# Two attention blocks instead of three, and eight of eleven sorted expert tiles returned through memory

## The chip, the cores and the metric

The kernel runs on one core of a Trainium2 chip. The metric is the device time of one execution in microseconds (us); the table below gives the median of three timed executions. TensorE is called PE, its weight loads PEld, VectorE DVE, ScalarE ACT, GpSimd POOL and SyncE SP, as in the profile. Each engine runs its own instructions in the order in which they are written, and semaphores order the engines among each other.

## The reference, cut to what matters

For 64 images, a small vision tower. The patches of each image go through a convolution; nine patches form a window and four windows a picture. Local attention (one query per window over its nine patches) gives four rows per image, and global attention over those four rows gives a class row. With one more token that makes six tokens of 256 numbers per image (384 rows in all, three tiles of 128). Then follow one transformer layer (layernorm, causal attention with 16 heads of 8 query numbers and 16 value numbers, output projection, residual) and a mixture of experts:

```
logits = layernorm(h) @ gate_w                       # 8 experts
p, idx = top_k(softmax(logits), 2);  p /= p.sum()
out_e  = (silu(x @ gate_e) * (x @ up_e)) @ down_e    # 512 hidden numbers
h      = h + sum over the two picks of p * out_e[idx]
```

All numbers are float32. Where accuracy asks for it, a float32 number is split into a high and a low part (names HI and LO), and a product is three matmuls (HI*HI, HI*LO, LO*HI).

## The kernel before, in words

**Up to the router.** The convolution of 18 tiles (six groups of three) feeds keys and values (`keys_values`, line 686: one pass of 512 columns makes the 256 key and the 256 value numbers of a tile). DVE scores windows (`window_scores`, L1778 and L1780; for the last three tiles one position at a time, `position_scores`, L1764 and L1766), takes the softmax and multiplies the values (`value_products`, L484). PE adds these nine products while it transposes them (`second_aggregate`, L754), projects (`local_rows`, L782), and makes the three row tiles in banks 6, 7 and 5: `patch_rows(0)` and `patch_rows(1)` (L799), and, after the softmax over the windows and its products (`global_scores` L809, `global_values` L819, `global_aggregate` L829), `class_rows` (L843). Each row tile is normalised (`row_moments`; ACT or DVE writes `inn`), turned (`turn_in`, L642), and multiplied by the query, key and value weights (`qkv`, L908). PE's order is written out by hand: for instance `qkv_cls` and the whole of `patch_rows(0)` stand before `second_aggregate`.

The attention among six tokens is done on DVE in blocks of queries. `BLOCKS` = (0,3), (3,5), (5,6): queries 0 to 2 over 3 keys (9 pairs), queries 3 and 4 over 5 keys (10 pairs), query 5 over 6 keys (6 pairs). For a block, `attention_products` (L505) multiplies 64 numbers for each pair, `att_dots` (L1984) adds them by head, `att_scores` (L1990, L1993) subtracts the maximum, ACT takes the exponential (L1380), `att_weights` (L2001, L2004, L2006) divides, and `token_values` (L496, on DVE and POOL) weighs the values. PE sums and turns these (`turn_context`, L754), projects them, and the router follows.

**From the router on.** Expert 0 is dense: all rows go through it. The picks of experts 1 to 7 are sorted by expert into 11 tiles of 128 rows (`SLOT_TILES`). Two tiles are gathered by one-hot matmuls; POOL scatters all rows into a memory tensor by six indirect transfers (`scatter`, L1647), and the other nine tiles are read from there into a ring of six (`tile_rows`, L466). The tile loop (lines 1169 to 1180 on PE) does in step s:

- `tile_gate_up(s)`: 12 matmuls of 512 columns (L1101) with expert weights split by ACT (`tile_weights_hi`, L1400) and DVE (`tile_weights_lo`, L2020);
- `rows_turn(s+1)` (L1086), then `tile_out(s-1)`, the down projection (L1121);
- `give_back(s-2)` (L1134): six matmuls with the one-hot matrix `back` that POOL makes (`way_back`, L1655), which add a tile's HI and LO rows into the three row tiles of the sum, in banks 4, 7 and 2. It needs `out_hi` on ACT (L1490) and `out_lo` on DVE (L2210);
- `hidden_turn(s)` (L1110), which needs ACT's silu (L1475) and DVE's `tile_product` (L2204); ACT's `hidden_copy` (L1482) follows.

SP loads the weights of a tile in two parts, 1024 KB (`tile_a`, L553) and 512 KB (`tile_b`, L560), into a ring of three. `tile_a(t)` waits until tile t-3 is split, `tile_b(t)` until `tile_out(t-3)` is done. After the loop PE adds the residual and the dense expert's rows (`add_repeated`, L1154, L1156), then the last tile (`last_give_back`: three HI matmuls, and three LO matmuls that wait for `out_lo(10)`), and ACT and DVE copy the sums out.

## Time and profile before

| what | value |
|---|---|
| three timed executions | 207.58, 206.12, 205.95 us (median 206.12) |
| the profiled execution | 204.24 us, of which the span of its instructions is 202.4 us |
| busy PE, PEld, DVE, ACT, POOL | 190.9, 166.0, 139.8, 105.4, 79.1 us |
| bytes moved | 32.90 MB |

The profiled execution is 1.88 us below the median of the timed ones, and its span leaves out 1.84 us around the first and the last instruction. All rows below are of that one execution, in us from the start of its span.

### The profile page before, as it was taken

The numbers are of one execution on the slowest core, as the hardware profiler recorded it, in microseconds if no ns is written. First come the engines' busy times: TensorE is split into PE (matmuls) and PEld (weight loads), VectorE is DVE, ScalarE is ACT, GpSimd is POOL, SyncE is SP. The second block draws the span as 40 slices with busy tenths as digits, with TensorE's granted clock in tenths as the row PEclk, the third lists the DMA queues.
The fourth block names the chain that finished last, engine by engine and source line by source line (L and its number), as shares of the span: only waits on it lengthen the run. The fifth ranks groups of instructions, "written<-read, shape, count | busy, mean of one in ns | idle before, by whom it ended". The sixth has DMA issues, their size and how long they took to land.

```text
span 202.4 us, 3427 instructions
## 1 busy us (share of the span) xinstructions
PE 190.9 (94%) x1123; PEld 166.0 (82%) x1123; DVE 139.8 (69%) x344; ACT 105.4 (52%) x233; POOL 79.1 (39%) x112
## 2 busy tenths in 40 slices
PE   8999999999999997999968799999999999999991
PEld 8898989998897875877747599888878888888881
DVE  1787983585999997745798869396496676766311
ACT  4366492645427444543842551473486676767331
POOL 6235076464474040359355536790032222102220
PEclk9999999999999999999999999999999999999998
DMA  6999997000491000000002900217999987923003
GB/s 214 358 389 367 361 343 236 2 0 3 143 410 70 3 0 0 0 2 0 3 0 71 429 21 2 102 55 195 419 394 377 360 284 290 317 96 108 0 0 78
DMA packets 10349, 32.90 MB, mean 163 GB/s; under 512 B 1222, under 2 KB 5788, under 8 KB 8668
## 3 DMA queue, kind: packets, MB, share of 16 engines
q1 hardware_dynamic: 8140, 29.53, 40.3%
q10 hardware_dynamic: 1904, 2.37, 3.6%
q0 software_dynamic: 288, 0.79, 1.1%
q8 instruction: 9, 0.15, 0.3%
q14 instruction: 8, 0.07, 0.1%
HBM read 30.05 MB, written 2.64 MB: 161 GB/s over the span
## 4 chain that ended last, share of the span: by engine, by line
PE 75%; DVE 18%; issue 3%; ACT 2%; POOL 0%; DVEq 0%; ACTq 0%; POOLq 0%
PE bank L1101 15%; PE bank L1121 9%; PE bank L597 8%; PE bank L695 6%; PE bank L618 6%; PE bank L1029 4%; PE bank L1134 4%; PE bank L1039 3%; PE bank L1110 2%; DVE stats L1724 2%; PE bank L642 2%; PE bank L605 2%; DVE kv_rows L1778 1%; DVE vprod L484 1%; DVE split L1882 1%
## 5 line engine op out<-in xcount | busy, mean ns | idle before, releaser
L1101 PE MATMUL bank<-split 128*128 128x512 f32 x132 | 33.4, 401 | 0.1
L1655 POOL TENSOR_SCALAR split<-token_row,window 128x384 fp32r<-128x384 f32 x11 | 15.1, 1372 | 46.5 <-PE bank L1134 46.5
L1101 PEld LDWEIGHTS bank<-split 128*128 128x128 f32 x132 | 24.0, 188 | 5.3 <-issue 0.3
L695 PE MATMUL bank<-split 128*128 128x512 f32 x108 | 26.5, 397 | 0.0
L1559 POOL TENSOR_TENSOR rstd<-veps,mhalf 128x1 f32<-128x1 f32 (+2 forms) x17 | 14.3, 844 | 28.1 <-DVE veps L1731 27.9
L2020 DVE TENSOR_TENSOR split<-raw,split 128x512 fp32r<-128x512 f32 x28 | 18.4, 695 | 6.7 <-ACT split L1400 6.6
L695 PEld LDWEIGHTS bank<-split 128*128 128x128 f32 x108 | 19.8, 188 | 3.9
L597 PE MATMUL bank<-split 128*128 128x256 f32 (+1 forms) x180 | 22.7, 285 | 0.0
L597 PEld LDWEIGHTS bank<-split 128*128 128x128 f32 (+1 forms) x180 | 22.1, 191 | 0.2
L1400 ACT CAST split<-raw 128x512 fp32r<-128x512 f32 x28 | 16.7, 619 | 2.8 <-DMA raw<-ffn_w 2.8
L1247 ACT ACTIVATE kv_rows<-bank,rstd 128x512 f32<-128x512 f32 x18 | 12.1, 688 | 10.1 <-PE bank L695 9.3
L2204 DVE TENSOR_TENSOR kv_rows<-bank,kv_rows 128x512 f32<-128x512 f32 x11 | 7.6, 691 | 12.3 <-PE bank L1101 9.1
L1579 POOL TENSOR_TENSOR window<-window,pe_rows 128x256 f32<-128x256 f32 x14 | 11.7, 838 | 9.3 <-ACT pe_rows L1196 8.6
L1196 ACT COPY pe_rows<-bank 128x256 f32<-128x256 f32 x18 | 6.3, 373 | 16.1 <-PE bank L597 15.5
L618 PE MATMUL bank<-split 128*128 128x256 f32 (+1 forms) x90 | 12.6, 296 | 0.0
L2020 DVE TENSOR_TENSOR split<-kv_rows,split 128x512 fp32r<-128x512 f32 x16 | 11.1, 733 | 1.9 <-ACT split L1400 1.9
L618 PEld LDWEIGHTS bank<-split 128*128 128x128 f32 (+1 forms) x90 | 11.7, 201 | 0.5 <-DVE split L1866 0.2
L1724 DVE BATCH_NORM_STATS2 stats<-pe_rows 128x6 f32<-128x256 f32 x18 | 6.5, 414 | 8.3 <-ACT pe_rows L1196 8.1
L1134 PE MATMUL bank<-split 128*128 128x256 f32 x60 | 10.5, 311 | 0.0
L1211 ACT CAST split<-raw 128x384 fp32r<-128x384 f32 (+1 forms) x15 | 6.7, 510 | 6.0 <-DMA raw<-xb 4.0
L1400 ACT CAST split<-kv_rows 128x512 fp32r<-128x512 f32 x16 | 9.5, 621 | 0.4 <-PE bank L1101 0.4
L1475 ACT ACTIVATE kv_rows<-bank 128x512 f32<-128x512 f32 x11 | 6.6, 599 | 5.7 <-PE bank L1101 5.7
(282 smaller groups left out, 401.7 us busy)
## 6 DMA issues: line engine op xcount, KB each, us to landing
raw<-ffn_w SPq DMA_DIRECT2D x7, 1024.0 KB, 7.7
kv_rows<-ffn_w SPq DMA_DIRECT2D x4, 1024.0 KB, 5.4
raw<-xa SPq DMA_DIRECT2D x5, 768.0 KB
raw<-ffn_w SPq DMA_DIRECT2D x7, 512.0 KB, 7.4
kv_rows<-ffn_w SPq DMA_DIRECT2D x4, 512.0 KB, 5.9
tok<-tok_w SPq DMA_DIRECT2D x1, 1536.0 KB, 12.5
raw<-ffn_w SPq DMA_DIRECT2D x1, 1536.0 KB, 6.8
expert_rows<-zero_row SPq DMA_DIRECT2D x1, 1419.0 KB, 15.8
```

The source lines that it names most:

```text
L597: mm = pe.matmul(bank[b][:, 0:C], xs[0:n, g % 2, px, a:a + P], cws[0:n, pw, k, :], start=(k == 0 and m == 0), stop=(k == len(KCH) - 1 and ...
L618: mm = pe.matmul(bank[GT * g + j][:, 0:C], xs[0:n, g, px, a:a + P], cws[0:n, pw, k, :], start=(k == 0 and m == 0), stop=last)
L695: mm = pe.matmul(bank[b][:, :], lns[:, g % 2, px, a:a + P], wkvs[:, pw, aw:aw + 2 * C], start=(c == 0 and m == 0), stop=(c == CC - 1 and m ...
L1101: mm = pe.matmul(bank[half][:, :], xst[:, s % 2, px, c * P:(c + 1) * P], tile_aws[s % 2][:, piece, pw, :], start=(c == 0 and m == 0), stop ...
L1121: mm = pe.matmul(bank[6][:, 0:C], hcols[s % 2][:, q * P:(q + 1) * P], b_ring[ring(s)][:, q, :], start=(q == 0), stop=(q == FQ - 1))
L1134: mm = pe.matmul(bank[SUM_BANK[j]][:, 0:C], back[:, s % 2, j * P:(j + 1) * P], eo[:, s % 2, px, :], start=(s == 0 and px == HI), stop=False)
L1247: act.activation(kv_rows[:, 0:wt + 2:wt + 1, n, :], bank[b][:, :].rearrange("p (k c) -> p k c", k=2), ACT.Identity, scale=rstd[:, k, i - G ...
L1400: act.copy(tile_aws[s % 2][:, piece, HI, :].rearrange("p (q n) -> p q n", q=FQ), a_ring[ring(s)][:, :, piece * P:(piece + 1) * P]).then_in ...
L1559: pool.tensor_tensor(rstd[0:parts, k, 0:n], veps[0:parts, k, 0:n], mhalf[0:parts, 0:n], ALU.pow).then_inc(rstd_done, 1)
L1579: pool.tensor_tensor(redsum[:, wt, :], pe_rows[:, wt, 0, :] if n == 1 else redsum[:, wt, :], pe_rows[:, wt, n, :], ALU.add).then_inc(sum_s ...
L1655: pool.tensor_scalar(back[:, s % 2, :], token_row[:, :], xr[:, s % ROW_RING, ROW_TOKEN:ROW_TOKEN + 1], None, ALU.is_equal).then_inc(back_d ...
L2020: dve.tensor_tensor(tile_aws[s % 2][:, piece, LO, :].rearrange("p (q n) -> p q n", q=FQ), a_ring[ring(s)][:, :, piece * P:(piece + 1) * P] ...
```

## The change

There are two attention blocks, (0,3) and (3,6); the second has 18 pairs, so there are 27 pairs in place of 25. Contexts are still turned in three lots: tokens 1, 2, 0; then 5; then 3 and 4. The last three tiles' keys are made ahead of their values (`last_keys`, `last_values`), and their scores go as one `window_scores(1, 2)`. PE's order up to the attention is another: `second_aggregate` comes straight behind the first window's rows, with `global_scores(0)` inside; `patch_rows` and parts of the global values fill in; and all turns of the three row tiles and all `qkv` products stand behind `class_rows`. `in1` is normalised on DVE, and POOL makes the roots of `in0` and `in1` behind three weight splits.

Of the 11 sorted tiles the first eight (`FAR`) are no longer added by matmuls. ACT writes their weighted rows to a ring of three buffers, SP stores each tile (131 KB) to a new memory tensor `far_out`, and after the eighth POOL fetches each token's two rows by six indirect transfers of 128 rows (a pick in a later tile fetches a row of zeros). DVE adds the fetched rows to the row tiles. Tiles 8 to 10 go by `give_back` as before. There is one more small table on POOL, one more 131 KB store of zeros, and the load semaphores of the patch groups are shared by ring slot.

```diff
-BLOCKS = [(0, 3), (3, 5), (5, 6)]
+BLOCKS = [(0, 3), (3, 6)]
+CTX_TOKENS = ((1, 2, 0), (3, 4), (5,))
+FAR = SLOT_TILES - 3
+OUT_RING = 3
+ORDER_BACK = (2, 1, 0)
...
         def tile_rows(eng, s):
             if s >= ROW_RING:
-                eng.wait_ge(back_done, s - ROW_RING + 1)
-                eng.wait_ge(tile_out_split, s - ROW_RING + 1)
+                eng.wait_ge(tile_out_hi, s - ROW_RING + 1)
...
+            sp.dma_start(far_out[FAR * P:, :], zero_row[:, 0:C]).then_inc(zeroed, 16)
...
+            def far_write(s):
+                sp.wait_ge(tile_out_hi, s + 1)
+                sp.dma_start(far_out[s * P:(s + 1) * P, :], out_ring[:, s % OUT_RING, :]).then_inc(far_written[s % OUT_RING], 16)
...
                 if s + 2 < SLOT_TILES:
                     tile_a(s + 2)
                 tile_b(s)
+                if s - 3 < FAR:
+                    far_write(s - 3)
...
-            keys_values_group(5)
+            last_keys()
+            first_aggregate()
+            last_values(0)
+            local_begin(0)
+            last_values(1)
+            class_keys_mean()
+            local_rows(0)
+            last_values(2)
...
-            first_aggregate()
-            local_begin(0)
-            class_keys_mean()
-            local_rows(0)
             local_columns(0)
+            second_aggregate()
+            local_begin(1)
+            local_rows(1)
+            global_value(0, 0)
+            local_columns(1)
+            global_value(0, 1)
+            global_scores(1)
             patch_begin(0)
             patch_rows(0)
-            global_scores(0)
+            for c in range(CC):
+                mm = global_value(1, c)
+            mm.then_inc(filled[4], 1)
+            patch_begin(1)
+            patch_rows(1)
+            global_aggregate()
+            class_begin()
+            class_rows()
+            turn_in(0)
             pe.wait_ge(att_in, 16)
             pe.wait_ge(tok_cols, 1)
             qkv("qkv_cls")
-            second_aggregate()
-            local_begin(1)
-            local_rows(1)
-            turn_in(0)
-            local_columns(1)
-            patch_begin(1)
-            global_scores(1)
-            patch_rows(1)
-            global_values()
+            turn_in(1)
             tile_qkv(0, "qkv0", 0)
-            global_aggregate()
-            class_begin()
-            class_rows()
-            turn_in(1)
+            turn_in(2)
             tile_qkv(0, "qkv0", 1)
-            tile_qkv(1, "qkv1", 0)
-            turn_in(2)
-            tile_qkv(1, "qkv1", 1)
+            tile_qkv(1, "qkv1")
             tile_qkv(2, "qkv_pool")
...
             def tile_out(s, between=None):
-                pe.wait_ge(*((tile_out_split, s) if s else (hid_done, DENSE * FQ)))
+                if s > FAR:
+                    pe.wait_ge(tile_out_split, s - FAR)
+                else:
+                    pe.wait_ge(*((tile_out_hi, s) if s else (hid_done, DENSE * FQ)))
...
-                if s > 1:
+                if s - 2 >= FAR:
                     give_back(s - 2)
...
             def add_repeated():
                 pe.wait_ge(repeat_done, 2)
-                pe.wait_ge(acc_done, RT + 1)
+                pe.wait_ge(returned, 2)
                 pe.matmul(bank[SUM_BANK[2]][:, 0:C], repeat, acc[:, 2, :], start=False, stop=False)
-                pe.wait_ge(acc_done, 2 * RT)
+                pe.wait_ge(returned, 4)
...
+            h_copy(0)
             h_copy(1)
-            in_normalise(1)
+            in_normalise(0)
+            hT_copy(0)
             h_copy(2)
             hT_copy(1)
+            qkv_copy("qkv_cls")
+            copy_pair(2, "in2", hT[:, T - 1, :, :, :].rearrange("p c s b -> p c (s b)"))
             qkv_copy("qkv0")
-            copy_pair(2, "in2", hT[:, T - 1, :, :, :].rearrange("p c s b -> p c (s b)"))
             qkv_copy("qkv1")
+            qkv_copy("qkv_pool")
             attention_exp(0)
-            qkv_copy("qkv_pool")
             tile_weights_hi(0, 0)
-            attention_exp(2)
+            attention_exp(1)
             tile_weights_hi(0, 1)
-            attention_exp(1)
...
             def out_hi(s):
                 act.wait_ge(tile_down, s + 1)
                 wait_rows(act, s)
-                if s >= 2:
-                    act.wait_ge(given, s - 1)
+                if s < FAR:
+                    if s >= OUT_RING:
+                        act.wait_ge(far_written[s % OUT_RING], 16 * (s // OUT_RING))
+                    act.activation(out_ring[:, s % OUT_RING, :], bank[6][:, 0:C], ACT.Identity,
+                                   scale=xr[:, s % ROW_RING, ROW_WEIGHT:ROW_WEIGHT + 1]).then_inc(tile_out_hi, 1)
+                    return
...
-            for s in range(SLOT_TILES):
-                way_back(s)
+            way_back(FAR)
+            way_back(FAR + 1)
+            pool.wait_ge(far_step, 2)
+            for k in range(OUT_RING):
+                pool.wait_ge(far_written[k], 16 * len(range(k, FAR, OUT_RING)))
+            for j in ORDER_BACK:
+                for i in range(PICKS):
+                    pool.indirect_dma_start(returned_rows[:, i, j, :], None, far_out,
+                                            bass.IndirectOffsetOnAxis(ap=far_row[:, i, j:j + 1], axis=0)).then_inc(rows_back, 16)
+            way_back(FAR + 2)
...
             attention_products(dve, 0, ("qkv_cls", "qkv0")).then_inc(qk_dve, 1)
             att_dots(0)
             att_scores(0)
-            attention_products(dve, 1, ("qkv_cls", "qkv0", "qkv1")).then_inc(qk_dve, 1)
             att_weights(0)
-            attention_products(dve, 2, ("qkv_pool", "qkv1")).then_inc(qk_dve, 1)
-            att_dots(2)
-            att_scores(2)
+            attention_products(dve, 1, ("qkv_cls", "qkv0", "qkv1", "qkv_pool")).then_inc(qk_dve, 1)
             att_dots(1)
             att_scores(1)
-            att_weights(2)
-            att_wait(2, ATT)
-            token_values(dve, 5, SHARE, T).then_inc(dve_values, 1)
             att_weights(1)
             att_wait(1, ATT)
+            token_values(dve, 5, SHARE, T).then_inc(dve_values, 1)
             values(4)
...
+            def add_returned(j):
+                dve.wait_ge(acc_done, 2 * RT)
+                dve.wait_ge(rows_back, PICKS * RT * 16)
+                for i in range(PICKS):
+                    if i:
+                        dve.wait_ge(returned, 2 * ORDER_BACK.index(j) + i)
+                    dve.tensor_tensor(acc[:, j, :], acc[:, j, :], returned_rows[:, i, j, :], ALU.add).then_inc(returned, 1)
...
+                if s == 2:
+                    far_rows()
-                if s:
+                if s > FAR:
                     out_lo(s - 1)
+            for j in ORDER_BACK:
+                add_returned(j)
             out_lo(SLOT_TILES - 1)
```

## Rows read from the trace of the kernel before

**Rows 1.** The page, part 1: busy time of each engine.
```profile
PE 190.9 (94%) x1123; PEld 166.0 (82%) x1123; DVE 139.8 (69%) x344; ACT 105.4 (52%) x233; POOL 79.1 (39%) x112
```
**Rows 2.** Chain that ended last, in time: start, length, instruction.
```profile
20.04 5.39 PE bank L597 x45
...
72.78 4.25 PE bank L695 x18
...
83.58 1.97 PE bank L754 x18
...
94.25 1.15 PE bank L843 x4
...
107.20 1.58 DVE window L496 x2
...
163.64 0.71 PE bank L1134 x6
```
**Rows 3.** Timeline of one steady tile step: start, length, engine, line.
```profile
161.75 1.89 PE L1121 MATMUL bank<-kv_rows,loT 128*128 128x256 f32 x8
161.79 0.69 DVE L2204 TENSOR_TENSOR kv_rows<-bank,kv_rows 128x512 f32<-128x512 f32 x1 [0.99 <-PE bank L1101]
...
163.27 0.88 PEld L1134 LDWEIGHTS bank<-split 128*128 128x128 f32 x6
...
163.68 0.47 ACT L1490 ACTIVATE split<-bank,window 128x256 fp32r<-128x256 f32 x1 [0.32 <-PE bank L1121]
164.09 0.46 PEld L1110 LDWEIGHTS bank<-con,kv_rows 128*128 128x128 f32 x4
...
164.54 3.02 PE L1101 MATMUL bank<-split 128*128 128x512 f32 x12
```
**Rows 4.** Timeline up to the attention, 78 to 108 us.
```profile
80.38 2.70 DVE L484 TENSOR_TENSOR vprod<-kv_rows,pn 128x768 f32<-128x768 f32 x3
...
97.52 0.38 ACT L1375 COPY kv_rows<-bank 128x256 f32<-128x256 f32 x1
...
97.96 1.44 PEld L908 LDWEIGHTS bank<-att,tok 128*128 128x128 f32 x8
...
100.24 0.83 DVE L505 TENSOR_TENSOR vprod<-kv_rows 128x640 f32<-128x640 f32 x1
...
101.58 0.23 DVE L2006 TENSOR_TENSOR kv_rows<-kv_rows,r 128x72 f32<-128x72 f32 x1
...
103.55 0.89 DVE L1984 TENSOR_REDUCE kv_rows<-vprod 128x80 f32<-128x720 f32 x1
...
105.71 0.69 DVE L496 TENSOR_TENSOR window<-kv_rows 128x512 f32<-128x512 f32 x1
```
**Rows 5.** Timeline of the tile loop's step 2.
```profile
145.61 0.68 DVE L2204 TENSOR_TENSOR kv_rows<-bank,kv_rows 128x512 f32<-128x512 f32 x1
...
146.35 0.66 PE L1110 MATMUL bank<-con,kv_rows 128*128 128x128 f32 x4
```
**Rows 6.** Windows, 10 us of the tile loop: the last three columns are PEclk, DMA share, GB/s.
```profile
140.00:150.00 10.00, 9.95 (x52) 7.91 (x50) 6.71 (x12) 6.77 (x15) 1.75 (x1) 1.00 0.99 387
```
**Rows 7.** Timeline from tile 7's rows to the end.
```profile
181.27 0.48 ACT L1490 ACTIVATE split<-bank,window 128x256 fp32r<-128x256 f32 x1 [0.32 <-PE bank L1121]
...
197.10 0.48 DVE L2210 SCALAR_TENSOR_TENSOR split<-bank,window,split 128x256 fp32r<-128x256 f32 x1 [3.34 <-ACT split L1490]
```
**Rows 8.** DMA issues: KB each, us from issue to landing.
```profile
kv_rows<-ffn_w SPq DMA_DIRECT2D x1, 512.0 KB, 3.4
...
expert_rows<-pe_rows,dest_row POOLq DMA_INDIRECT x6, 2.7
...
window<-expert_rows SPq DMA_DIRECT2D x4, 129.0 KB, 3.5
```
**Rows 9.** Timeline of POOL's six indirect scatters: the first and the last.
```profile
125.47 1.24 POOL L1647 DMA_INDIRECT expert_rows<-pe_rows,dest_row  x1 [1.10 <-DVE pe_rows L2184]
...
132.28 0.96 POOL L1647 DMA_INDIRECT expert_rows<-pe_rows,dest_row  x1 [0.30 <-issue]
```

More of the change, by code:

```diff
@@ L88 @@
 GATE_COLS = GATE_COPIES * E
-QKV = {"qkv_cls": (7, (0,)), "qkv0": (0, (1, 2)), "qkv1": (1, (3, 4)), "qkv_pool": (4, (5,))}
+QKV = {"qkv_cls": (3, (0,)), "qkv0": (0, (1, 2)), "qkv1": (1, (3, 4)), "qkv_pool": (4, (5,))}
 def columns(items):
@@ L697, in keys_values, with last_products, last_keys, last_values @@
                 mm.then_inc(filled[b], 1)
+            def last_products(i, part):
+                g, j = divmod(i, GT)
+                b = 4 + i % KV_BANKS
+                for c in range(CC):
+                    for m, (px, pw) in enumerate(PRODUCTS):
+                        a, aw = (c * GT + j) * P, (2 * c + part) * C
+                        mm = pe.matmul(bank[b][:, part * C:(part + 1) * C], lns[:, g % 2, px, a:a + P], wkvs[:, pw, aw:aw + C],
+                                       start=(c == 0 and m == 0), stop=(c == CC - 1 and m == 2))
+                return mm
+            def last_keys():
+                for c in range(CC):
+                    wait_copied(pe, 2 + c, f"turn{GROUPS - 1}")
+                for i in range(TILES - GT, TILES):
+                    wait_free(pe, 4 + i % KV_BANKS, f"kv{i}")
+                    last_products(i, 0).then_inc(last_keys_full, 1)
+            def last_values(j):
+                i = TILES - GT + j
+                pe.wait_ge(last_keys_copied, j + 1)
+                last_products(i, 1).then_inc(filled[4 + i % KV_BANKS], 1)
             def class_column():
@@ L1134, in give_back @@
                         mm = pe.matmul(bank[SUM_BANK[j]][:, 0:C], back[:, s % 2, j * P:(j + 1) * P], eo[:, s % 2, px, :],
-                                       start=(s == 0 and px == HI), stop=False)
+                                       start=(s == FAR and px == HI), stop=False)
                 mm.then_inc(given, 1)
@@ L1542, in _ @@
             table(trash[:, :, :], [[RT * P, PICKS], [P, RT]], SLOTS + 1, 1)
+            table(last_row[:, :, :], [[0, PICKS], [0, RT]], FAR * P, 1)
             table(tile_no[:, :], [[1, SPILL]], 0, 0)
```

178 lines of the change are left out of this document (101 added, 77 removed).

## The prediction

> **What bounds the kernel now.** I read the busy times first: PE is busy for 190.9 us of the 202.4 [rows 1], so a matmul taken away may be time taken away, but only where PE is what ends last. The chain of waits says where. From the router to the end it is PE nearly without a break, tile step after tile step; in the window scores and in the attention it is DVE, and a busy PE there is not the limit. So the change is two changes: 48 matmuls leave a stage that PE bounds, and a new order comes into a stage that passes between PE, ACT and DVE. The timelines of these stages give the prices.
>
> **The stage up to the router.** A matmul of 256 columns takes 5.39 / 45 = 0.12 us [rows 2]. Before, the last three tiles' keys and values end at 72.78 + 4.25 = 77.03 [rows 2]. Now the 18 key halves come first, 18 x 0.12 = 2.2 us, and end at 75.0, 2.0 earlier. Against that DVE scores three positions at once (a product and a sum of 768 columns, about 1.0 each by 0.83 for 640 [rows 4]) and not only the last (256 columns, 0.33 each): 1.3 later. An ACT copy of 256 columns (0.47, nearest row L1490 [rows 3]) is shorter than one of 512. Together about 1 us: the value products that ran from 80.38 for 2.70 [rows 4] run from 79.4 to 82.1. `second_aggregate` ended at 83.58 + 1.97 = 85.55 [rows 2], because PE had other work first; now only its last third (0.66) stands behind the products: 82.8, which is 2.7 earlier. The global softmax and its sums follow 2.7 earlier, less about 0.2, as DVE takes the moments of two row tiles ahead of the class sum. `class_rows` ended at 95.40 [rows 2] and now ends near 92.9.
>
> Then the order takes back most of it. Before, one turn and one token's product stood between `class_rows` and the end of `qkv0`; now there are three turns (two instructions each) and three products. One product is 1.44 / 2 = 0.72 and an instruction 0.18 [rows 4], so 3 x 0.36 + 3 x 0.72 = 3.2 us, until 96.1. Four copies on ACT (the longest 0.38 [rows 4]; about 1.1) end at 97.2, against 97.52 + 0.38 = 97.90 before: 0.7 earlier.
>
> From there block 0's weights ended 3.9 us later, at 101.81 [rows 4], with block 1's product (0.83 from 100.24 [rows 4]) in the way, about half of which covered the exponential. Without it 3.5: 100.7. Block 1 now has 18 pairs: a product of 1152 columns, 0.83 x 1152 / 640 = 1.5; sums over 1296 columns, 0.89 x 1296 / 720 = 1.6 [rows 4]; maximum, difference, exponential, sum, reciprocal and product on 48 to 144 columns, six times about 0.3 (72 columns took 0.23 [rows 4]); ends and starts between them 0.2: 105.8. The value products (0.69 [rows 4] and 1.58 [rows 2]) end at 108.1, against 108.78 before: **0.7 us gained**. Everything from there to the tile loop is unchanged and moves with it. Bounds: 0.6 lost, if ACT's copies of `qkv_cls` and `in2`, which are now queued ahead of those of `qkv0`, cost their full 1.3; 1.9 gained, if the turns and products find their inputs ready and the wide DVE operations cost less than in proportion.
>
> With one answer: the further POOL table, the shared load semaphores and the 131 KB of zeros (queued behind the store of zeros that is there already, which nobody waits for until the scatters) are priced at nothing: POOL waits for the first convolution weights right after its tables. Were the table uncovered, it would be some 0.2 us.
>
> **The tile loop.** From the first load of `give_back` to the first load of `hidden_turn` are 164.09 - 163.27 = 0.82 us; the chain charges 0.71, the loads themselves 0.88 [rows 2, 3]. I take 0.82. What is late next? `hidden_turn` needs DVE's product, which ends at 161.79 + 0.69 = 162.48; PE now comes for it at 163.27, so 0.8 us stay over. ACT's `hidden_copy` would follow at once, and ACT's output row ends at 163.68 + 0.47 = 164.15 [rows 3]; the copy is wanted only after the next 12 matmuls (3.0 us). So 0.82 is won in full in a steady step.
>
> But not in step 2: there DVE's product runs from 145.61 to 146.29, since it stands behind a weight split that waited for tile 3's load, and `hidden_turn` follows at 146.35 [rows 5]. `give_back(0)` was hidden, and its removal is worth nothing. Steps 3 to 7 lose `give_back(1)` to `give_back(5)`: 5 x 0.82 = **4.1 us** (3.6 to 4.4). Those of steps 8 and 9 come after `tile_out(7)` on PE and belong to the end, below.
>
> DVE's `out_lo` (0.48 [rows 7]) and POOL's one-hots of eight tiles go too; neither was late. The waits added: SP waits for `out_hi` before each store, and the next `tile_a` is queued behind it, but that one waits a step longer anyhow. ACT waits for a store made three steps, some 15 us, before. The DMA queues now carry 1.57 MB of weights, 0.13 of rows and 0.13 of stores in a step, 1.84 MB; at the 387 GB/s of a full stretch [rows 6] that is 4.75 us, and a step will be (164.09 - 146.35) / 3 = 5.9 [rows 3, 5] less 0.82, 5.1. Close, but it holds.
>
> **The end.** The fetches hang on tile 7 alone. In the clock of before (everything so far only shifts it), ACT's row 7 ends at 181.75 [rows 7]. SP has by then issued the last 512 KB of weights (3.4 us from issue to landing [rows 8]); the store is queued behind and I give it 3.4 us as well: 185.2. POOL's six indirect scatters started (132.28 - 125.47) / 5 = 1.36 apart [rows 9] and landed 2.7 after issue [rows 8]; six fetches need 5 x 1.36 + 2.7 = 9.5: 194.7, and 0.1 for the wait. Six additions on DVE, 0.46 each with the start of the next (nearest row: `out_lo`, also 256 columns, 0.48 [rows 7]), end at 197.6. `out_lo(10)` stands behind them on DVE and ends at 198.1. Before it ended at 197.10 + 0.48 = 197.58 [rows 7]. What follows it (three matmuls, two copies, the stores) is unchanged. So the end comes **0.5 us later** in that clock, and the two `give_back`s of steps 8 and 9 win nothing, because PE would be ready at 197.58 - 1.64 = 195.9. Bounds: 1.6 earlier, if the rows are back in time; 2.2 later, with 3.5 us for landing (another kind of small transfer [rows 8]: 0.8 more) and a pitch of 1.54 (0.9 more).
>
> For that pitch: the first scatter, beside a weight split on DVE, took 1.24, the last 0.96 [rows 9]. The Trainium skill (SBUF — State Buffer, "Who interferes with whom") says that DVE's two-port operations (it names copies, casts and operations with a scalar) lock GpSimd out while it makes descriptors, and that an operation on two tensors takes only the reading side. By that rule the weight splits would not slow the fetches, and the sum stays. If the first scatter's 1.24 is such a block all the same, a pitch of 1.24 + 0.30 makes the six 5 x 0.18 = 0.9 us longer.
>
> **Sum.** -0.7 - 4.1 + 0.5 = -4.3 us. The profiled execution's 204.24 becomes 199.9; the median of the timed ones, 1.88 higher, becomes 206.12 - 4.3 = **201.8**, and that is the forecast. One percent, about what a measurement of this kernel can tell from no change, is 2.06 us: faster is below 204.06, slower above 208.18.
>
> **Rivals.**
> - *The rows are back in time.* If a fetch is issued every 1.0 us, PE sets the end: 201.8 - 0.5 - 1.6 = 199.7. Against it: the last scatter's own 0.96 and the gap of 0.30 before it make 1.26 [rows 9]. Chance 0.13.
> - *The attention order wins nothing.* What `second_aggregate` gains is lost at PE's queue behind `class_rows` and at the wide second block, whose exponential nothing covers: 201.8 + 0.7 to + 1.3, near 202.8. Chance 0.15.
> - *The step does not shrink.* If stores and loads together get 313 GB/s, 1.84 MB need 5.9 us and weights set the pace: 206.12 - 0.7 + 0.5 = 205.9, at 340 GB/s some 203.5. For it: the full stretch before, and a step 2 that waited for a load. Against: later in the loop the loads run ahead. Chance 0.09.
> - *The fetches go one by one, and the kernel is slower.* If each of the six must land before the next is issued, they need 6 x (2.7 + 0.3) = 18 us, not 9.5, and nothing but three tiles covers them: 201.8 + 8.5 = 210.3. It decides from a pitch of 1.36 + 4.3 / 5 = 2.2 us on. Against it: the scatters' pitch is half of their landing time, so they overlapped. Chance 0.08.
> - The forecast, within about 1.3 us: 0.55.
>
> **Range and chances.** Best bounds together would be -1.9 - 4.4 - 1.6 = -7.9, worst (without a rival) +0.6 - 3.6 + 2.2 = -0.8. For eight in ten I take 199.2 to 204.6; it leaves out the slow fetches, the worst of the weights, and the joint best. Faster by over 1 percent: 0.55 + 0.13 + 0.12 + 0.02 = 0.82. Within 1 percent: 0.10. Slower: 0.08.
>
> **What would show it.** `second_aggregate` ends near 82.8 and `class_rows` near 92.9, but the copy of `qkv0` ends only near 97.2; block 1's product is one instruction of 1152 columns and 1.5 us; the last value product ends near 108.1. A steady tile step takes 5.0 to 5.1 us with PE never idle, step 2 as long as before. From the end of row 7 to the first fetch are some 3.5 us, the fetches start 1.36 apart, DVE idles before the first addition, and PE idles between `tile_out(10)` and the last LO matmuls for about 2 us. The prediction is wrong if the fetches start 2 us or more apart, if ACT's weight casts wait for loads in steps 4 to 9, or if the value products end after 109.5.

## The result, and the profile after

The changed kernel takes **202.82 us** (median of 12 runs, 201.52 to 205.27); the kernel before, timed beside it, 205.75 (204.82 to 207.58). The ratio is **0.986, interval 0.9832 to 0.9888**: 2.9 us faster. The forecast of 201.8 had the sign and its range held the time, but it promised 4.3 us. The profiled execution took 202.39 us, its span is 200.6.

First the page's busy times, for [rows 1]:

```profile
PE 185.6 (93%) x1093; PEld 161.3 (80%) x1093; DVE 138.5 (69%) x334; ACT 105.2 (52%) x234; POOL 74.6 (37%) x110
```

30 matmuls net are gone (48 of the way back, less 18 more because the last three tiles' keys and values are now separate passes), PE's busy time fell by 5.3 us and the span by 1.8. To see where that time went, a fixed point is needed first, because two executions of the same kernel don't begin alike. I take the start of the third patch group's convolution on PE, the 45 matmuls that stand first in [rows 2]. They began at 20.04 us before and at 21.55 after; ahead of them the change only adds the table on POOL and shares the load semaphores. In the thirteen profiles of this study this point lies between 20.04 and 23.01 us, in two of the changed kernel itself at 21.55 and 22.89. It hangs on the landing of the first loads: ACT's first splits waited 1.23 us for a patch load before and 2.85 after. The profile of before was lucky by 1.5 us, so I count all times from this point. The chain of waits of the kernel before (start, length, what), at the points that bound the pieces below:

```profile
115.13 2.19 PE bank L946 x18
...
140.71 3.04 PE bank L1101 x12
...
147.01 2.97 PE bank L1101 x12
...
176.52 2.77 PE bank L1101 x12
```

And of the changed kernel (for [rows 2], [rows 5] and [rows 7]):

```profile
21.55 5.38 PE bank L615 x45
...
93.21 1.13 PE bank L885 x4
...
107.58 2.61 DVE window L507 x3
...
116.55 2.19 PE bank L994 x18
...
142.19 3.02 PE bank L1147 x12
...
147.60 2.77 PE bank L1147 x12
...
173.42 2.77 PE bank L1147 x12
...
178.68 3.69 DMA far_out<-tok
...
189.95 2.81 DMA tok<-far_out,far_row
```

Read it by differences, in pieces that begin and end at the same work in both kernels:

| piece | before | after | change | forecast |
|---|---|---|---|---|
| fixed point to the end of the last value products | 88.74 | 88.64 | -0.10 | -0.7 |
| from there to the router's first matmul (115.13 before, 116.55 after) | 6.35 | 6.36 | 0 | 0 |
| router to tile 7's output row on ACT | 66.62 | 62.10 | -4.52 | -4.1 |
| tile 7's row to the end of the last `out_lo` | 15.83 | 17.08 | +1.25 | +0.5 |
| from there to the end of the span | 4.82 | 4.87 | +0.05 | 0 |
| sum | 182.36 | 179.05 | **-3.3** | -4.3 |

(88.74 is 107.20 + 1.58 - 20.04 [rows 2], 88.64 is 107.58 + 2.61 - 21.55.) The sum of -3.3 is near the -2.9 of the medians; the two spans alone would say -1.8. (The forecast itself was counted from the median of three executions, 206.12; twelve give 205.75.)

The attention of the changed kernel, in the timeline (start, length, engine, line, operation; for [rows 4]):

```profile
98.62 0.38 ACT L1446 COPY kv_rows<-bank 128x256 f32<-128x256 f32 x1
...
102.38 1.36 DVE L516 TENSOR_TENSOR vprod<-kv_rows 128x1152 f32<-128x1152 f32 x1
...
107.62 2.29 POOL L507 TENSOR_TENSOR window<-kv_rows 128x256 f32<-128x256 f32 x2 [2.25 <-DVE kv_rows L2083]
```

Block 1's product of 1152 columns took 1.36 (1.5 forecast) and its sums 1.50 (1.6). The copy of `qkv0` ends at 98.62 + 0.38 = 99.00, which is 97.49 in the clock of before, where the fixed point lies 1.51 earlier (97.2 forecast, 97.90 before). `class_rows` ends at 93.21 + 1.13 - 1.51 = 92.83 (92.9 forecast). What was not forecast is the last line and its partner in the chain: VectorE's three value products took 2.61 us, beside GpSimd's two.

And the end, in the timeline of the changed kernel from tile 7's row on (for [rows 7]):

```profile
178.18 0.47 ACT L1562 ACTIVATE tok<-bank,window 128x256 f32<-128x256 f32 x1 [0.32 <-PE bank L1170]
...
178.31 0.33 SPq L572 DMA_DIRECT2D kv_rows<-ffn_w  x1
...
183.25 1.38 POOL L1797 DMA_INDIRECT tok<-far_out,far_row  x1 [15.54 <-DMA far_out<-tok]
...
192.12 0.47 ACT L1567 ACTIVATE split<-bank,window 128x256 fp32r<-128x256 f32 x1 [2.08 <-PE bank L1170]
192.86 2.48 DVE L2296 TENSOR_TENSOR pe_rows<-pe_rows,tok 128x256 f32<-128x256 f32 x6 [3.57 <-DMA tok<-far_out,far_row]
...
195.25 0.48 DVE L2302 SCALAR_TENSOR_TENSOR split<-bank,window,split 128x256 fp32r<-128x256 f32 x1
```

Tile 7's row is ready at 178.18 + 0.47 = 178.65, the store is issued at 178.68 and lands 3.69 later (the row of the chain above), and GpSimd issues the first fetch at 183.25: 4.6 us after the row, where 3.5 were forecast. The fetches start (189.95 - 183.25) / 5 = 1.34 apart (1.36 forecast), and the first addition starts 9.61 after the first fetch (9.6). The six additions take 2.48 (2.76). `out_lo` of the last tile stands behind them on DVE: it starts 3.13 us after ACT's part of the same tile (195.25 against 192.12).

### The profile page after: what moved, and what is told of

The parts are those of the page before. It is cut to its first block, busy times and chain, and to the rows that moved or that the text cites. A ratio compares the mean times of both kernels' runs of the same rounds, so it can differ in the third digit from the quotient of the medians.

```text
span 200.6 us, 3342 instructions
## 1 busy us (share of the span) xinstructions
PE 185.6 (93%) x1093; PEld 161.3 (80%) x1093; DVE 138.5 (69%) x334; ACT 105.2 (52%) x234; POOL 74.6 (37%) x110
## 3 DMA queue, kind: packets, MB, share of 16 engines
q0 software_dynamic: 576, 1.58, 2.5%
## 4 chain that ended last, share of the span: by engine, by line
PE 57%; DVE 22%; DMA 6%; issue 5%; ACT 3%; POOL 3%; POOLq 0%; ACTq 0%; DVEq 0%
PE bank L1147 13%; PE bank L615 8%; PE bank L1170 7%; PE bank L636 4%; PE bank L713 4%; PE bank L1075 4%; DMA raw<-xa 3%; PE bank L1085 3%; PE bank L660 2%; DVE kv_rows L1855 2%; DVE stats L1808 2%; POOL tok L1797 2%; DMA far_out<-tok 2%; DVE vprod L495 2%; PE bank L1156 2%
## 5 line engine op out<-in xcount | busy, mean ns | idle before, releaser
L1147 PE MATMUL bank<-split 128*128 128x512 f32 x132 | 33.3, 401 | 0.0
L1147 PEld LDWEIGHTS bank<-split 128*128 128x128 f32 x132 | 24.0, 188 | 5.2 <-DVE split L2269 0.3
L713 PE MATMUL bank<-split 128*128 128x512 f32 x90 | 22.1, 397 | 0.0
L713 PEld LDWEIGHTS bank<-split 128*128 128x128 f32 x90 | 16.4, 188 | 3.3
L1657 POOL TENSOR_TENSOR window<-window,pe_rows 128x256 f32<-128x256 f32 x14 | 13.0, 930 | 9.2 <-ACT pe_rows L1245 8.4
L1733 POOL TENSOR_SCALAR split<-token_row,window 128x384 fp32r<-128x384 f32 x3 | 3.8, 1255 | 30.6 <-DMA window<-expert_rows 30.5
L1296 ACT ACTIVATE kv_rows<-bank,rstd 128x512 f32<-128x512 f32 x15 | 10.0, 689 | 7.5 <-PE bank L713 6.6
L1797 POOL DMA_INDIRECT tok<-far_out,far_row x6 | 6.1, 1020 | 17.1 <-DMA far_out<-tok 15.5
L2097 DVE TENSOR_TENSOR split<-kv_rows,split 128x512 fp32r<-128x512 f32 x16 | 10.3, 685 | 2.7 <-ACT split L1470 2.7
```

Source lines behind the costliest of these rows:

```text
L713: mm = pe.matmul(bank[b][:, :], lns[:, g % 2, px, a:a + P], wkvs[:, pw, aw:aw + 2 * C], start=(c == 0 and m == 0), stop=(c == CC - 1 and m ...
L1147: mm = pe.matmul(bank[half][:, :], xst[:, s % 2, px, c * P:(c + 1) * P], tile_aws[s % 2][:, piece, pw, :], start=(c == 0 and m == 0), stop ...
L1296: act.activation(kv_rows[:, 0:wt + 2:wt + 1, n, :], bank[b][:, :].rearrange("p (k c) -> p k c", k=2), ACT.Identity, scale=rstd[:, k, i - G ...
L1657: pool.tensor_tensor(redsum[:, wt, :], pe_rows[:, wt, 0, :] if n == 1 else redsum[:, wt, :], pe_rows[:, wt, n, :], ALU.add).then_inc(sum_s ...
L1797: pool.indirect_dma_start(returned_rows[:, i, j, :], None, far_out, bass.IndirectOffsetOnAxis(ap=far_row[:, i, j:j + 1], axis=0)).then_inc ...
L2097: dve.tensor_tensor(tile_aws[s % 2][:, piece, LO, :].rearrange("p (q n) -> p q n", q=FQ), a_ring[ring(s)][:, :, piece * P:(piece + 1) * P] ...
```

## Experiments

All are changed at one place from the changed kernel, except where it is said. Ratios are to the kernel before, run on the same chip.

**The two halves of the change alone, and a repetition.** `attn_only` has the new order and the two attention blocks, and all tiles go back through PE as before. `far_only` has the order and the three blocks of before, and eight tiles over memory:

```diff
 # far_only
-BLOCKS = [(0, 3), (3, 6)]
+BLOCKS = [(0, 3), (3, 5), (5, 6)]
 ...
 FAR = SLOT_TILES - 3
```

> The first half of the change alone: two attention blocks and the new order up to the router, with all eleven tiles given back by matmuls as before. Theory: the order wins almost nothing, because the value products of block 1 on DVE and POOL disturb each other; counted from the class-key matmuls (so that the first loads do not enter) the last value product ends 0.1 to 0.3 us earlier than before, and the time is 0.999 of before (0.995 to 1.003). Rival, the forecast's own price: 0.7 us earlier, 0.9965. Rival: the order loses, and the whole gain is the loop's: above 1.003.

Measured: **0.9995** (0.9966 to 1.0024), 205.14 us against 205.47.

> The second half alone: eight tiles back over memory, with the attention and its order as before. Theory: a tile step of 5.16 us in place of 5.86, five or six of them won before tile 7's rows, and 1.2 us given back at the end: 2.3 to 3.1 us faster, 0.985 to 0.989 of before. Rival: something early in the kernel (the further table, the store of zeros) costs the 1.5 us that the changed kernel's profile shows in its first 10 us; then the class-key matmuls start near 73.3 us here and near 71.7 us in the run with the attention alone, and the time is nearer to 0.993.

Measured: **0.9892** (0.9852 to 0.9933), 203.47 us.

> The changed kernel once more, as the control of this series. Theory: 0.986 of before (0.983 to 0.989); the first loads land at another time than in its first profile, so that the class-key matmuls start between 71.5 and 73.5 us. Rival: they start at 73.3 again, because the change delays the first loads.

Measured: **0.9882** (0.9837 to 0.9926), 203.69 us. The rival of `far_only`, that the table or the store of zeros delays the start, asked for class-key matmuls near 73.3 us there and near 71.7 in `attn_only`, which has neither. They began at 73.27 and at 73.20, so neither is the cause. In `after_again` they began at 74.61, outside the 71.5 to 73.5 that I expected. Nor is the late start a standing cost of the change: 1.5 us would be 0.7%, and `attn_only`, whose fixed point lies at 21.48, takes 0.9995 of before and at most 1.0024.

All the gain is in the tiles over memory. The order is worth nothing that a time can tell, and what the profiles tell is the same each time: value products end 88.55 after the fixed point in `attn_only`, 88.64 in `after_again`, and 88.78 with three blocks in `far_only`. That is 0.1 to 0.2 us. In `attn_only` even that was lost behind it. Its windows (length, busy time of PE, PEld, DVE, ACT, POOL with their counts; the last three columns are granted clock, DMA share, GB/s):

```profile
106.00:108.00 2.00, 0.43 (x3) 0.29 (x2) 1.61 (x4) 1.66 (x4) 0.55 (x1) 0.71 0.00 0
108.00:110.00 2.00, 2.00 (x6) 1.53 (x6) 2.00 (x4) 0.00 (x0) 1.75 (x2) 0.50 0.00 0
```

and its chain, with three rows that are used further below (the last is of its timeline, tile 7's output row on ACT):

```profile
21.48 5.38 PE bank L601 x45
...
117.68 2.19 PE bank L980 x18
...
143.32 3.02 PE bank L1133 x12
...
149.43 2.80 PE bank L1133 x12
...
183.53 0.47 ACT L1544 ACTIVATE split<-bank,window 128x256 fp32r<-128x256 f32 x1 [0.32 <-PE bank L1153]
```

TensorE had 0.43 us of matmuls in the 2 us from 106 to 108, while it waited 1.57 us for ACT's copy of the first turned contexts, which stood behind two weight splits on ACT. From near 107 us it was granted half its clock, 1.2 instead of 2.4 GHz, until 113 to 114 us, just when the products came. The router began 117.68 - 21.48 = 96.20 after the fixed point, 1.1 later than the 95.09 of before. The same half clock stands in this stretch in six of the ten profiles with two blocks and in none of the three with three. What it costs goes with its length. In slices of 1 us the profile shows it for some 6.8 us in `attn_only` and in `store_first`, below, where the router came 96.41 after the fixed point, 1.3 late; for some 3.4 us in the other four, and there the router came at 94.87 to 95.08, not late. The short wait alone doesn't bring it: the profile of the changed kernel has the same one and keeps the full clock:

```profile
106.00:108.00 2.00, 0.42 (x4) 0.18 (x3) 1.51 (x5) 1.73 (x4) 0.38 (x1) 1.00 0.00 0
```

**Seven tiles over memory.** If each step gains some 0.7 and the end loses because tile 7's row comes back too late, one tile less in memory should cost one step and free the end:

```diff
-FAR = SLOT_TILES - 3
+FAR = SLOT_TILES - 4
 ...
             way_back(FAR + 2)
+            way_back(FAR + 3)
```

> The changed kernel with seven tiles over memory and four by matmuls: the fetches start a whole step earlier, and one more give-back lies in the loop. Theory (the end hangs on the fetches, PE waits about 2 us for them): the rows are back before PE comes for them, PE sets the end, and against the changed kernel 5.2 us of waiting for the fetches is swapped for 0.7 us of matmuls: the last LO row ends 1.5 to 2.2 us earlier, 0.976 to 0.980 of before. Rival (the end is set by something else, or the fetches only begin to collide with the weight loads): no gain against the changed kernel, 0.985 to 0.99.

Measured: **0.9785** (0.9741 to 0.9829), 200.71 us.

> The kernel with seven tiles over memory once more, beside the one with six on the same chip. If 0.9785 was the kernel and not the chip or the moment: 0.975 to 0.982. If the changed kernel's 0.988 and this differ by the moment only, 0.985 or more. In its profile PE should have no wait ahead of the six additions.

Measured: **0.9789** (0.9754 to 0.9823), 201.22 us. The end of `far7_again` in the timeline:

```profile
190.34 2.61 DVE L2297 TENSOR_TENSOR pe_rows<-pe_rows,tok 128x256 f32<-128x256 f32 x6 [0.15 <-DMA tok<-far_out,far_row]
...
193.02 0.47 ACT L1567 ACTIVATE split<-bank,window 128x256 fp32r<-128x256 f32 x1 [2.08 <-PE bank L1170]
...
193.53 0.48 DVE L2303 SCALAR_TENSOR_TENSOR split<-bank,window,split 128x256 fp32r<-128x256 f32 x1 [0.57 <-ACT split L1567]
```

The first fetch goes out at 180.61, the additions start at 190.34 with 0.15 of waiting, and `out_lo` of the last tile starts 0.51 after ACT's part (193.53 against 193.02), not 3.13. That gives 2.6 us back; the step that again has its `give_back` takes 0.7. From the fixed point to the end it is 177.1 us, against 179.05 in the changed kernel. This version beats both kernels.

**Six tiles.**

```diff
-FAR = SLOT_TILES - 3
+FAR = SLOT_TILES - 5
 ...
             way_back(FAR + 2)
+            way_back(FAR + 3)
+            way_back(FAR + 4)
```

> The changed kernel with six sorted tiles over memory and not eight (rows of tiles 6 to 10 go back by the one-hot product on PE; the other six are stored, fetched and added as before). Theory A (each tile over memory takes 0.70 us of PE out of the loop, and the end waits only when the last stored tile is the eighth): against the kernel with seven, which came to 0.9785, one step of 5.16 us becomes 5.88, nothing at the end is gained, and the ratio is 0.980 to 0.984. Theory B (the fetches still hold the end with seven, or they disturb the loop's weight loads there): six is as fast as seven or faster, 0.974 to 0.979. PE waits for no addition in either.

Measured: **0.9793** (0.9763 to 0.9823), 201.46 us, beside 201.22 with seven. The time doesn't separate the theories: the difference of 0.24 us is inside the intervals, and 0.9793 lies a little under theory A's range. The chain does, in the first matmuls of three steps running:

```profile
168.31 2.77 PE bank L1147 x12
...
173.46 2.77 PE bank L1147 x12
...
179.33 2.76 PE bank L1147 x12
```

173.46 - 168.31 = 5.15 us without `give_back`, 179.33 - 173.46 = 5.87 with it: 0.72 for a tile. From the fixed point to the end it is 199.4 - 21.62 = 177.8 us, against 198.9 - 21.80 = 177.1 in `far7_again`. So six costs what theory A says in the profile. The timed difference is smaller, but with intervals of some 0.6 us either way on each kernel it excludes neither 0.7 us nor nothing.

**Why the store lands late: another queue.** In the changed kernel the store of tile 7's row is issued 0.37 us behind the last 512 KB of weights on the same queue.

```diff
             def far_write(s): ...
-                if s - 3 < FAR:
+                if s - 3 < FAR - 1:
                     far_write(s - 3)
 # on ACT, behind the activation of tile FAR - 1
+                        act.wait_ge(tile_out_hi, s + 1)
+                        act.dma_start(far_out[s * P:(s + 1) * P, :], out_ring[:, s % OUT_RING, :])
```

> The changed kernel, with one DMA issued elsewhere: the store of tile 7's output rows goes out on ScalarE's queue, right behind the activation that writes them, and no longer on SP's queue behind the last 512 KB weight load. In the two profiles of the changed kernel the store was issued 0.03 to 0.04 us after those rows were ready, landed 3.69 and 3.73 us after that, and the first fetch began 0.88 to 0.9 us later (178.68 to 183.25, 180.04 to 184.65); the six additions then ended 2.4 us before the last row's product could be taken in, so that the end came 1.2 us later than without the eight rows in memory. Theory A (the store stands behind the last weights in the queue and on the DMA engines): it lands in 2.0 to 2.8 us, the first fetch begins some 1 to 1.7 us sooner, PE's wait of 1.8 us ahead of the additions falls to under 0.8, and the ratio to the kernel before goes from 0.988 to 0.981 to 0.985. Theory B (a store of 128 KB takes this long by itself, or all queues share the DMA engines with the weights): it lands after 3.4 to 3.9 us as before, and the ratio stays at 0.986 to 0.990. A cost of the edit in both: ScalarE issues a DMA, 0.1 to 0.6 us, ahead of its next split.

Measured: **0.9863** (0.9834 to 0.9893), 202.85 us. In the timeline and, last, the chain of `store_act`:

```profile
177.45 0.47 ACT L1562 ACTIVATE tok<-bank,window 128x256 f32<-128x256 f32 x1 [0.32 <-PE bank L1170]
...
177.95 0.33 ACTq L1566 DMA_DIRECT2D far_out<-tok  x1
...
182.48 1.42 POOL L1800 DMA_INDIRECT tok<-far_out,far_row  x1 [15.55 <-DMA far_out<-tok]
```

```profile
177.95 3.65 DMA far_out<-tok
```

On a queue of its own the store took 3.65 us, and the first fetch began 4.56 after the row (182.48 - 177.92). Theory A is wrong: the queue is not what it waits in. Theory B left two causes together. The packets say when the store moved (queue, packets, MB, share of 16 engines; q1 is SP's queue, q10 ACT's). First all that moved from 177.9 to 180.5 us, then the store from 180.5 to 182:

```profile
q1 hardware_dynamic: 115, 0.44, 74.6%
```

```profile
q10 hardware_dynamic: 144, 0.13, 25.1%
```

For 2.5 us behind its issue no packet of the store moved, though it had a queue to itself; its 0.13 MB went when 0.10 MB of the load was left.

**Why the store lands late: ahead of the weights.** The same queue, the two issues in the other order:

```diff
             for s in range(3, SLOT_TILES):
                 ...
+                if s == SLOT_TILES - 1:
+                    far_write(s - 3)
                 tile_b(s)
-                if s - 3 < FAR:
+                if s < SLOT_TILES - 1 and s - 3 < FAR:
                     far_write(s - 3)
```

> The changed kernel with two DMAs of SP in the other order: the store of tile 7's rows is issued ahead of the last 512 KB weight load and no longer 0.35 us behind it. With the store on another queue it still landed 3.65 us after its issue, at the moment when the weights landed as well. Theory A (what it waits for is the weights' data on the DMA engines, which all queues share): ahead of the weights the store lands in 2.1 to 2.8 us (64 KB alone at the end of these kernels take 2.1), the first fetch begins 0.9 to 1.5 us sooner, the additions and the end follow by as much, less what is then late instead (the second half of the last tile's product), and the ratio goes from 0.988 to 0.982 to 0.985. Theory B (128 KB into memory with its receipt take this long alone): it lands after 3.4 us or more and the ratio stays at 0.985 to 0.990. The weights land 0.4 us later in both, with over 8 us to spare ahead of the last tile's second product.

Measured: **0.982** (0.9768 to 0.9872), 202.11 us against 205.26. The profiled execution had a lower mean clock (0.973), all of it ahead of 118 us, so I read it only behind the router. Its chain and the end of its timeline:

```profile
181.55 1.72 DMA far_out<-tok
```

```profile
181.04 0.48 ACT L1564 ACTIVATE tok<-bank,window 128x256 f32<-128x256 f32 x1 [0.32 <-PE bank L1172]
...
184.14 1.07 POOL L1799 DMA_INDIRECT tok<-far_out,far_row  x1 [13.56 <-DMA far_out<-tok]
...
194.99 0.47 ACT L1569 ACTIVATE split<-bank,window 128x256 fp32r<-128x256 f32 x1 [2.08 <-PE bank L1172]
...
196.03 0.48 DVE L2304 SCALAR_TENSOR_TENSOR split<-bank,window,split 128x256 fp32r<-128x256 f32 x1
```

The store lands in 1.72 us, not 3.69; the first fetch begins 2.62 after the row (184.14 - 181.52), not 4.6; `out_lo` starts 1.04 after ACT's part, not 3.13. From tile 7's row to the end of `out_lo` it is 14.99 us, 2.1 less than in the changed kernel and 0.8 less than before. So what held the store was the load that had been issued ahead of it, on its own queue or on the other. The Trainium skill (DMA: Bandwidth & Descriptors, "Queues, rings and completion order") says that SP's and ACT's queues have one ring each on the same sixteen DMA engines, and that an engine goes round the queues that have work, packet by packet. The shared engines fit: another queue 3.65 us, another order 1.72. The turn by turn doesn't show: by it the store's packets in `store_act` should have gone among the load's, and they went at its end. Whether it was the load's data that they waited for, or something ahead of the engines, no run here separates. The size of the move is a miss of mine: I expected 0.9 to 1.5 us, and with it 2.1 to 2.8 us for the store alone, by stores of 64 KB that take 2.1 at the end of these kernels.

**Why the value products took 2.61: VectorE alone.** Block 1's value products all on VectorE, none on GpSimd; the waits of PE and SP that counted GpSimd's two go with them:

```diff
-            token_values(pool, 5, 0, SHARE).then_inc(pool_values, 1)
-            token_values(pool, 3, 0, SHARE).then_inc(pool_values, 1)
 ...
-            token_values(dve, 5, SHARE, T).then_inc(dve_values, 1)
+            token_values(dve, 5, 0, T).then_inc(dve_values, 1)
 ...
-            token_values(dve, 3, SHARE, 4).then_inc(dve_values, 1)
+            token_values(dve, 3, 0, 4).then_inc(dve_values, 1)
```

> The changed kernel, with the second attention block's value products all on VectorE and none on GpSimd (in the changed kernel GpSimd takes 256 columns of each of two, 2.29 us for both, beside three of VectorE's). In the changed kernel VectorE's three (512, 384 and 512 columns) take 2.61 us, where the same kind took 0.69 us for 512 and 0.82 for 640 in other places of the trace: 1.9 to 2.0 us by these. Theory A (the two engines slow each other when both read two operands from the on-chip memory): alone on its ports VectorE takes its three, now of 768, 640 and 512 columns, in 0.96 + 0.82 + 0.69 = 2.4 to 2.5 us, so the second block's values are ready 0.1 to 0.3 us sooner than now though VectorE does 512 columns more; the ratio moves by under 0.002. Theory B (no contention, VectorE's pace of 1.85 ns per column in this stretch is its own): 1920 columns take 3.6 us, the values are ready 0.9 to 1.0 us later, and the ratio rises by 0.004 to 0.005.

Measured: **0.981** (0.9768 to 0.9851), 202.53 us. The groups by form on VectorE, first of the changed kernel, then of `vals_dve` (out<-in, count | busy, mean ns of one):

```profile
L507 DVE TENSOR_TENSOR window<-kv_rows 128x640 f32<-128x640 f32 x1 | 1.2, 1243 | 0.0
L507 DVE TENSOR_TENSOR window<-kv_rows 128x256 f32<-128x256 f32 x1 | 0.8, 836 | 0.0
L507 DVE TENSOR_TENSOR window<-kv_rows 128x512 f32<-128x512 f32 x1 | 0.7, 693 | 0.0
```

```profile
L507 DVE TENSOR_TENSOR window<-kv_rows 128x640 f32<-128x640 f32 x1 | 0.8, 819 | 0.0
L507 DVE TENSOR_TENSOR window<-kv_rows 128x512 f32<-128x512 f32 x1 | 0.7, 684 | 0.0
```

(The three are of 512, 640 and 256 columns in this order; the expectation has them as 512, 384 and 512, which is the same sum.) 640 columns take 1243 ns in the midst of GpSimd's products and 819 alone; 256 in their midst take 836, more than 640 alone. With 512 columns more VectorE ends sooner: 88.33 after the fixed point, not 88.64. The Trainium skill (SBUF — State Buffer, "Who interferes with whom") says that a VectorE operation with two inputs in this memory contends with a GpSimd instruction that reads it. The rows agree for two of the three; the first, of 512 columns, took 693 ns though GpSimd's product ran beside nearly all of it (684 alone). So did the 640 of the kernel before, which began 0.05 us ahead of a GpSimd product and took 824: in these rows, what VectorE has begun first is not slowed, and what it begins during a GpSimd product is. The prediction had cited this place for the fetches and not applied it here. The time that this freed was not seen at the router: it began 95.08 after the fixed point (116.84 - 21.76), as before, with the clock at 0.50 to 0.64 from 108 to 112 again. The ratio is lower than the 0.986 to 0.988 of the changed kernel, more than theory A allowed; the span counted from the fixed point is 178.9 (200.7 - 21.76) against 179.05, so the profile has no cause for that, and the intervals overlap.

**The two together, and the old order with seven tiles.** `far7_vals` is `far7` with the value products of `vals_dve`; `far7_old` is `far_only` with `FAR = SLOT_TILES - 4`.

> Seven tiles over memory (ratio 0.979 twice), and the second block's value products all on VectorE. If what this freed in the profile (values ready 0.3 us sooner) passes on to the router: 0.976 to 0.979. If the stage ahead of the router gives it back, as when TensorE's granted clock stands at half in the stretch behind the values (then the router began no sooner): 0.978 to 0.982. A step above 0.984 would speak against both.

Measured: **0.981** (0.9763 to 0.9857), 200.89 us against 205.26. The router came 94.87 after the fixed point, 0.1 sooner than in `far7_again`, with half clock from 106 to 110; the second reading is nearer, though the interval holds both.

> Seven tiles over memory with the order and the three attention blocks of the kernel before. Theory A (the new order and the two blocks bring the router 0.1 us sooner and no more, by the profiles so far: value products ended 88.74 us after the first keys and queries before, 88.55 to 88.66 with two blocks): the ratio is that of seven tiles with the new order, 0.977 to 0.982. Theory B (the forecast: the order is worth 0.7 us): 0.982 to 0.985. Rival C (the two blocks cost time, since TensorE's clock falls to half behind the values in some executions, and in none with three blocks): 0.974 to 0.977.

Measured: **0.9782** (0.9742 to 0.9822), 200.62 us. Its chain:

```profile
21.76 5.39 PE bank L614 x45
...
108.90 1.58 DVE window L506 x2
...
116.83 2.19 PE bank L963 x18
```

Value products end 108.90 + 1.58 - 21.76 = 88.72 after the fixed point (what the expectation calls the first keys and queries is this convolution), the router begins at 95.07 (95.01 in `far7` and `far7_again`). Theory A: in the profiles the new order and the two blocks bring 0.1 us. 0.7 of them would have shown as 0.982 or more, which is the interval's upper end; rival C's 0.977 lies in the interval too, but `far7` and `far7_again` lose nothing by the two blocks at the router.

## Why the prediction was right, and where its sizes were off

**Right: what carries the gain, and what eats it.** 48 matmuls left a stage that PE bounds, the step shrank, and nothing took their place there. DVE was not late, and `class_rows`, `second_aggregate` (84.47 - 1.51 = 82.96; 82.8 forecast), the fetches' pitch and the wait of DVE ahead of the additions came as told. The rivals of slow fetches and of a step that doesn't shrink did not happen. Of the latter something is there in single executions: in `far_only` a load of 8.0 us, in `far7` one of 6.9 and in `far7_vals` one of 5.1 stand in the chain in the loop's first steps; by the start of the step behind it, counted from the router, they cost 0.6, 1.3 and 0.5 us.

**The term of a step, 0.82.** Five steps, from the first matmul of tile 3 to that of tile 8, took 176.52 - 147.01 = 29.51 us before and 173.42 - 147.60 = 25.82 after: 0.74 a step, and 0.72 in a steady one (5.15 against 5.87, both in the trace of `far6`). I had taken the distance between two weight loads, 0.82. The chain had charged 0.71 [rows 2], and it was right: the weight loads overlap the matmuls, so the distance of the next load is not what PE's matmuls give back. 3.7 instead of 4.1, and 0.2 of that is one long step of before (6.06 us, the other four 5.86).

**The step that I called worth nothing.** "`give_back(0)` was hidden, and its removal is worth nothing" was wrong. Tile 2's first matmul to tile 3's took 147.01 - 140.71 = 6.30 us before and 147.60 - 142.19 = 5.41 after: 0.89 gained. I had read DVE's product, which ended 0.06 ahead of `hidden_turn` [rows 5], as something that holds still. It hung on a load that landed late in that execution, and after the change it was done sooner. `attn_only`, which still has `give_back(0)`, took 149.43 - 143.32 = 6.11 us there: 0.7 of the 0.89 is the `give_back`, 0.2 the late load. From the router to tile 7's row `attn_only` took 183.53 + 0.47 - 117.68 = 66.32 us, 0.3 less than that one execution of before; against it the six steps gave 4.2, and the sum of the pieces is -3.0, nearer to the medians. A step that was left out and a step that was priced too high nearly cancel, so that the piece came out near its forecast is luck.

**The stage up to the router, -0.7.** It gave -0.1. Half of the miss is in the value products, forecast as 0.69 + 1.58: the three took 2.61 and not 2.27, since the 640 columns, which began ahead of GpSimd's product before (824 ns), now begin in the midst of it (1243); alone VectorE does more columns in 2.29 (`vals_dve`). The other 0.3 is ahead of it: the copy of `qkv0` ended 0.4 sooner, not 0.7, though `class_rows` ended when forecast. It lies in PE's queue behind `class_rows`, whose products are in the chain of the changed kernel:

```profile
94.56 0.76 PE bank L957 x4
...
95.80 0.76 PE bank L957 x4
...
97.03 0.86 PE bank L957 x4
```

From the end of `class_rows` at 94.34 to 97.03 + 0.86 = 97.89 are 3.55 us, where the prediction added up 3.2: it priced a product at 0.72 by half of a row of weight loads, and the products took 0.76 to 0.86, with two waits of 0.07 between them. ACT's four copies took the 1.1 forecast, and from there to the value products it was 8.6 us (107.58 - 99.00), as forecast. So the rival "the attention order wins nothing" is what happened in this stage, and half of it by the mechanism that it named, PE's queue; the wide second block was not to blame. That its 202.8 meets the measured median is chance, as step 2 and the end are in that number too.

**The end, +0.5.** It was +1.25. The term that was mis-sized is the way from tile 7's row to the first fetch, "the store is queued behind and I give it 3.4 us as well": the store took 3.69 to land, and the fetch was issued 0.88 after that, for which the sum had nothing; the additions gave back 0.3. The larger part of the miss is the 0.88. It is the same wherever the store stood (0.88 in `store_act`, 0.87 in `store_first`), and no run here takes it apart. The store's place behind the load is another matter: the forecast had its price nearly right but took it for given, and `store_first` shows that one line of order is worth 2 us there in the profile. The sum by the measured terms is -0.1 - 4.5 + 1.3 = -3.3.

**Open.** Why the first loads land so differently that the fixed point lies between 20.04 and 23.01 us; why the clock falls to half behind the two blocks in six of ten executions, and for 6.8 us in two of them; what fills the 0.88 us between a store's landing and the fetch; and why `vals_dve` was timed faster than its profile explains.

## What to carry to other kernels

Work that is moved off the bounding engine to memory must be back before that engine's end: the last piece decides, and one tile fewer (0.72 us of PE) saved 2.6 us at the end. A small store that someone waits for is issued ahead of a large load that nobody waits for yet; another queue did not help here. And count both profiles from a point ahead of the change before subtracting them: here that point alone moved by up to 3 us.

## What the runs showed of the hardware

- A store of 128 KB to memory landed in 1.72 us ahead of a 512 KB load, in 3.69 behind it on the same queue, in 3.65 issued behind it on another. On the other queue none of its packets moved for 2.5 us.
- VectorE's product of two operands in on-chip memory, 640 columns: 819 ns alone, 824 begun just ahead of a GpSimd product, 1243 begun during one; 512 columns 684 alone and 693 begun just ahead.
- TensorE's granted clock fell to half in the attention, behind a stretch of waits (0.43 us of matmuls in 2 us in `attn_only`), in six of ten executions with the two-block order: for some 3.4 us in four, which cost nothing, and for some 6.8 us in two, which cost 1.1 and 1.3 us. The changed kernel's own profile had the same waits (0.42 us in 2) and kept the full clock.
